# Layernorm, softmax-weighted attention and an integer-weight MLP on one core: block 0's rows in four transfers, its bias seeds on TensorE, the weight check on 16-bit copies, and six low halves moved to GpSimd

## What is computed

```
xn   = layernorm(x)                               # (2, 4096, 256)
h    = tanh(xn @ W1.T + b1);  s = h @ w2 + b2     # one score per token
e    = exp(s - max(s));  ctx = cumsum(e*xn)/cumsum(e)
out1 = tanh(concat(ctx, xn) @ Wc.T + bc)
out2 = (silu(xn @ wg.T/127) * (xn @ wu.T/127)) @ wd.T/127   # wg, wu 768x256, wd 256x768, integers -127..127
y    = x + out1 + out2
```

## Time and profile before

| | us |
|---|---|
| median of 3 runs (lowest, highest) | 399.24 (398.85, 399.65) |
| the profiled execution | 400.47 |
| its span, first to last instruction | 398.6 |
| TensorE busy in the span | 389.4 |
| VectorE, ScalarE, GpSimd busy | 295.6, 252.4, 198.2 |

### The profile page before, as it was taken

The page is one execution under the profiler, slowest core; times in us unless marked ns, Lnnn a source line. Parts: engine busy times, 40 slices in busy tenths (PEclk is TensorE's granted clock), DMA queues, the critical chain, the costliest instruction groups (busy, mean ns, idle before and its releaser), DMA issues.

```text
span 398.6 us, 7885 instructions
## 1 busy us (share of the span) xinstructions
PE 389.4 (98%) x2741; PEld 270.6 (68%) x2741; DVE 295.6 (74%) x629; ACT 252.4 (63%) x469; POOL 198.2 (50%) x257
## 2 busy tenths in 40 slices
PE   7979999999999999999999999999999999999995
PEld 3546766675667488677686876767758677686765
DVE  5998899999785889897666846689766776745351
ACT  4988787999797666975536574456353644626250
...
DMA packets 54612, 36.44 MB, mean 91 GB/s; under 512 B 31651, under 2 KB 49956, under 8 KB 54565
## 3 DMA queue, kind: packets, MB, share of 16 engines
...
...
## 4 chain that ended last, share of the span: by engine, by line
PE 91%; ACT 3%; DVE 3%; issue 1%; DMA 1%; DVEq 0%; ACTq 0%
PE bank L659 43%; PE bank L695 38%; PE bank L715 9%; ACT rows L879 1%; DMA xres<-in_x 1%; ACT xnat L809 0%; ACT ex L845 0%; DVE stats L913 0%; DVE bank L1053 0%; DVE bank L1068 0%; ACT sg L838 0%; PE bank L652 0%; DVE wide L1073 0%; DVE xnat L983 0%; PE bank L1288 0%
## 5 line engine op out<-in xcount | busy, mean ns | idle before, releaser
L695 PE MATMUL bank<-xt,narrow 128*128 128x512 f16 x768 | 176.7, 379 | 0.1
L695 PEld LDWEIGHTS bank<-xt,narrow 128*128 128x128 f16 x768 | 75.2, 98 | 77.3 <-DVE erT L1035 0.6
L659 PE MATMUL bank<-narrow,xt 128*128 128x256 f16 x768 | 94.8, 277 | 1.8 <-ACT bank L792 1.8
L659 PE MATMUL bank<-narrow,wide 128*128 128x256 f16 x792 | 96.3, 273 | 0.0
L659 PEld LDWEIGHTS bank<-narrow,xt 128*128 128x128 f16 x768 | 76.1, 100 | 19.3 <-ACT bank L792 2.2
L659 PEld LDWEIGHTS bank<-narrow,wide 128*128 128x128 f16 x792 | 77.4, 98 | 9.4
L838 ACT ACTIVATE sg<-bank 128x512 f32<-128x512 f32 x96 | 56.6, 594 | 39.7 <-PE bank L695 37.2
L1190 POOL TENSOR_TENSOR wide<-ex,wide 128x512 f16<-128x512 f32 x32 | 41.2, 1301 | 71.7 <-ACT wide L859 71.7
L1073 DVE TENSOR_TENSOR wide<-bank,wide 128x512 f16<-128x512 f32 x90 | 60.5, 682 | 20.7 <-ACT wide L845 19.1
L1068 DVE SCALAR_TENSOR_TENSOR bank<-bank,sg 128x512 f32<-128x512 f32 x96 | 65.4, 692 | 13.8 <-PE bank L695 13.0
L845 ACT ACTIVATE wide<-bank 128x512 f16<-128x512 f32 x90 | 53.1, 594 | 33.8 <-DVE bank L1068 32.7
...
## 6 DMA issues: line engine op xcount, KB each, us to landing
...
xt<-xt SPq DMA_TRANSPOSE x56, 2.5
wide<-in_wg SPq DMA_DIRECT2D x1, 768.0 KB, 5.9
wide<-in_wu SPq DMA_DIRECT2D x1, 768.0 KB, 7.5
wide<-in_wd SPq DMA_DIRECT2D x1, 768.0 KB, 10.2
...
```

The lines of the kernel that those rows point to most:

```text
L659: return pe.matmul(dst, lhs, rhs, start=False, stop=stop, skip_group_check=True)
L695: mm = pe.matmul(b[:, :], pg.up(which, k, j), pg.xn(sx, k, tok), start=n == 0, stop=n == len(todo) - 1)
```

## The change

1. **Block 0's x.** It came as two transfers of 256 KB (one issued by SyncE, one by ScalarE) and now comes as four of 128 KB (two by each). The biases and w2 are issued by ScalarE's queue behind them, and no longer by SyncE's. The statistics of the four tiles are taken in the order 0, 2, 1, 3, then all four are aggregated together. `WARM` goes from 13 to 12.
2. **Block 0's seeds.** `Ss` of block 0 is gone from ScalarE; TensorE writes the bias with two f32 matmuls of one row and 256 columns per pair, ahead of the pair's `S`.
3. **The integer checks.** They read the f32-sized integer weights, on ScalarE (four passes, `Kg` and `Kd`) and VectorE (`Ku`, `Ke`). They now read the f16 copies that GpSimd has made: VectorE clears the sign bit of wg and wu together (`Kg`, 3072 values), takes maxima of halves (`Kh` 1536, `Ku` 768), the same for wd (`Kd` 1536, `Ke` 768), and ScalarE compares the 768 left of each (`Kx`, `Ky`).
4. **Block 0's low halves.** For the six (0, j), `H` writes its f32 product into unused SBUF in place of the bank, which so comes free at `H`; `Hh` reads it there, and GpSimd makes the low half (`Hm`) instead of VectorE's `Hl`.
5. The planner's start times, some due times and the needs follow, so all orders are computed anew.

```diff
-BEGIN = {TE: 8.3, SE: 6.5, VE: 8.9, PO: 1.0, SY: 12.0}
+LOW_ON_POOL = tuple((0, j) for j in range(KH))
+BEGIN = {TE: 7.6, SE: 5.8, VE: 8.1, PO: 1.0, SY: 12.0}
...
             def scores(i, pr):
                 b = bank_of(pg, "S", i, pr)
-                pe.wait_ge(a_ss, pg.nth("Ss", i, pr))
+                if i or pg.wide:
+                    pe.wait_ge(a_ss, pg.nth("Ss", i, pr))
+                else:
+                    open_bank(pe, pg, "S", i, pr)
+                    for t in range(2):
+                        pe.matmul(b[:, t * D:(t + 1) * D], ups[:, :], b_row[:, 0:D],
+                                  start=t == 0, stop=False, skip_group_check=True)
...
-            elif kind in ("Kg", "Kd"):
-                w, done = (wg32, 0) if kind == "Kg" else (wd32[:, WD_SHARE:], 2)
-                act.wait_ge(s_wg if kind == "Kg" else s_wd, 16)
-                if done + n:
-                    act.wait_ge(a_ok, done + n)
-                beyond = rows[:, :, :, :].rearrange("p r k t -> p (r k t)").bitcast(BF16)[:, 0:w.shape[1]]
-                act.activation(beyond, w.bitcast(I32), ACT.Relu, bias=limit[:, 0:1], scale=-1.0 if n else 1.0,
-                               accum_out=guard[:, 2 + done + n:3 + done + n]).then_inc(a_ok, 1)
+            elif kind in ("Kx", "Ky"):
+                n, up = (0, 1.0) if kind == "Kx" else (1, 1.0 / WD_DOWN)
+                act.wait_ge(v_k2, 5 if n else 3)
+                if n:
+                    act.wait_ge(a_ok, n)
+                act.activation(beyond(), largest(2 * n), ACT.Relu, bias=limit[:, 0:1], scale=up,
+                               accum_out=guard[:, 2 + n:3 + n]).then_inc(a_ok, 1)
...
+        def stats_first(dve):
+            for t in (0, 2, 1, 3):
+                dve.wait_ge(s_x0[t], 16)
+                ins = dve.bn_stats(stats[:, t, :], xres[:, t, :])
+            ins.then_inc(v_bn, 2)
+            dve.wait_ge(v_bn, 2)
+            for t in range(4):
+                ins = dve.bn_aggr(mv[:, t, :], stats[:, t, :])
+            ins.then_inc(v_mv, 2)
...
+            elif kind in ("Kg", "Kd"):
+                first, n, w = (0, 4, narrow[:, 0:2 * n_int]) if kind == "Kg" else (2, 2, wd16)
+                dve.wait_ge(g_w, 2 if kind == "Kg" else G_W)
+                if kind == "Kd":
+                    dve.wait_ge(v_k2, 3)
+                dve.tensor_scalar(largest(first, n).bitcast(U16), w.bitcast(U16), NO_SIGN, None,
+                                  ALU.bitwise_and).then_inc(v_k2, 1)
+            elif kind == "Kh":
+                dve.wait_ge(v_k2, 1)
+                dve.tensor_tensor(largest(0, 2), largest(0, 2), largest(2, 2), ALU.max).then_inc(v_k2, 1)
             elif kind == "Ku":
-                dve.wait_ge(s_wu, 16)
-                check_reduce(dve, 6, wu32.bitcast(I32), AX.X).then_inc(v_k, 1)
+                dve.wait_ge(v_k2, 2)
+                dve.tensor_tensor(largest(0), largest(0), largest(1), ALU.max).then_inc(v_k2, 1)
...
+            elif kind == "Hm":
+                pool.wait_ge(a_h, pg.nth("Hh", i, k))
+                m = KH * i + k
+                pool.tensor_tensor(half(pg.h(1, m, slice(0, BLK))), up_full(i, k), half(pg.h(0, m, slice(0, BLK))),
+                                   ALU.subtract).then_inc(g_h, 1)
```

More of the change, by code:

```diff
@@ L113, in closing @@
         return ("Ct" if seeded(i, x) else "Ca"), i, x
+    if kind == "Gu" and (i, x) in LOW_ON_POOL:
+        return "H", i, x
     return CLOSES[kind], i, x
@@ L157, in due_times @@
             for n, i in enumerate(blocks):
-                lead = 6.0 if i == FIRST_T else 10.0
+                lead = 9.0 if i == FIRST_T else 10.0
                 due["B", i, 0], due["B", i, 1] = first - lead + 2.0 * n, first - lead + 1.0 + 2.0 * n
@@ L161, in due_times @@
                     due["Lx", i, 0] = first - 18.0 + 2.0 * n
-            root = first - (8.5 if FIRST_T in blocks else 8.5)
+            root = first - (11.5 if FIRST_T in blocks else 8.5)
             due["R", g, 0] = root
@@ L173, in due_times @@
             due["Xl", i, pr] = end["Lb", i, pr] + 0.8
-            due["Ss", i, pr] = due["S", i, pr] - (1.6 if i or not pr else 0.6)
+            due["Ss", i, pr] = due["S", i, pr] - 1.6
             due["Th", i, pr], due["Sv", i, pr] = end["S", i, pr] + 0.1, end["S", i, pr] + 0.8
@@ L262, in needs @@
     if kind == "S":
-        return [(("Ss", i, x), 0), ((*turned, x), 0.8 if turned[0] == "Xl" and not wide else 0),
+        return [*([(("Ss", i, x), 0)] if i or wide else []), ((*turned, x), 0.8 if turned[0] == "Xl" and not wide else 0),
                 *([] if turned[0] == "Tx" else [(("Xh", i, x), 0)]), *([] if i else [(("W1l", 0, 0), 0.4)])]
@@ L267, in needs @@
     if kind == "Sv":
-        return [(("Th", i, x), 0)]
-    if kind == "Ss" and i == 0 and not wide:
-        return [(("Ea", 0, 0), 0), *([(("Xh", 0, 0), 0)] if x else [])]
+        return [(("Th", i, x), 0), *([] if i or x else [(("Ea", 0, 0), 0)])]
+    if kind == "Ss":
+        return [(("Ea", 0, 0), 0)]
     if kind in ("Gg", "Gu"):
@@ L279, in needs @@
         return [(("H", i, x), 0), *slot]
-    if kind == "Hl":
+    if kind in ("Hl", "Hm"):
         return [(("Hh", i, x), 0)]
     if kind == "D":
-        return [(("Hl", i, k), 0.2 * k) for k in range(KH)] + ([(("Ct", i, x), 0)] if seeded(i, x) else []) \
+        return [(("Hm" if (i, k) in LOW_ON_POOL and not wide else "Hl", i, k), 0.2 * k) for k in range(KH)] + ([(("Ct", i, x), 0)] if seeded(i, x) else []) \
             + [(("D", i, 0) if x else ("Wdh", 0, 0), 0)]
@@ L318, in may_precede @@
     kind, i, _ = st
-    return kind in WEIGHTS + ONCE or (kind in AHEAD and i < (1 if kind in ("Hh", "Hl", "D") else 2))
+    return kind in WEIGHTS + ONCE or (kind in AHEAD and i < (1 if kind in ("Hh", "Hl", "Hm", "D") else 2))
 class Plan:
@@ L410, in take_one @@
                 self.times.add(t)
-            elif opened(st) is None or self.bank_for(st, now) is not None:
+            elif opened(st, self.wide) is None or self.bank_for(st, now) is not None:
                 self.start(e, st, now)
@@ L752, in tensor_step @@
                 pe.wait_ge(a_b, 1)
-                pe.matmul(bank_of(pg, "Kp", 0, 0)[:, 0:1], ones[:, :], guard[:, 8:9], start=True,
+                pe.matmul(bank_of(pg, "Kp", 0, 0)[:, 0:1], ones[:, :], guard[:, 4:5], start=True,
                           stop=True).then_inc(p_ok, 1)
@@ L1067, in vector_step @@
                 dve.wait_ge(p_u, pg.nth("Gu", i, n))
-                dve.scalar_tensor_tensor(out=dst, in0=b[:, :], scalar=pg.up_scale, in1=sg[:, m % SG_RING, :],
+                dve.scalar_tensor_tensor(out=up_full(i, n) if pg.low_on_pool(i, n) else half(dst), in0=half(b[:, :]),
+                                         scalar=pg.up_scale, in1=half(sg[:, m % SG_RING, :]),
                                          op0=ALU.mult, op1=ALU.mult).then_inc(v_h, 1)
@@ L1317, in _ @@
             dve.memset(warm[:, 0:BLK], 1.0).then_inc(v_set, 1)
+            dve.memset(ups[:, :], X_UP * W_UP)
             dve.memset(ones[:, :], 1.0).then_inc(v_set, 1)
-            for pr in range(2):
-                vector_stats(dve, 0, pr)
+            stats_first(dve)
             root_first(dve)
```

115 lines of the change are left out of this document (70 added, 45 removed).

## The result

| | before | changed |
|---|---|---|
| median of 14 runs each, us (lowest, highest) | 399.60 (398.85, 403.54) | 404.19 (401.72, 409.13) |
| ratio to before, 95% interval | | 1.0084 (1.0047 to 1.0121) |
| profiled execution: time, span | 400.47, 398.6 | 403.58, 401.8 |

The change made the kernel slower by 0.8%; the forecast was 396.2, and the range ended at 399.0. The ratio is over the fast executions alone: the four of the changed kernel from 408.75 to 409.13 us are left out of it, and with them the medians are 1.1% apart. The page of the changed kernel answers to the earlier trace rows: TensorE is as busy as before, in a span 3.2 us longer.

A forecast was written before the change was run, and what follows sets the result against it. TensorE, busy 389.4 of 398.6 us, was taken as the bound. Start +0.7, seeds −2.0 and between the blocks +4.3 made 3.0 us gained, taken off the median 399.24 to give 396.2; range 395.2 to 399.0.

The forecast's parts named there:

- Start, +0.7: Block 0's x in four pieces lets statistics and transposes start earlier: 0.7 us gained, bounds 0.08 to 0.77.
- Seeds, −2.0: Block 0's four new f32 seed matmuls lie on TensorE's dense path: 2.0 us lost (1.5 to 2.25).
- The rival with a second fall of the clock: Clock falls again despite shorter waits: gain only 0.4 us, 398.8 us; chance 0.08.
- 16-bit steps: VectorE's five new integer-check steps, priced at 1.05, 0.95, 0.55, 0.6 and 0.55 us.
- That rival: 16-bit steps run at 1.04 ns an element, 5.1 us more: 403.2 us, or 400.6 without a clock fall; chance 0.07.
- Between the blocks, +4.3: From block 0's gate and up to the branch: 4.3 us gained, 2.7 from the clock, 1.6 from less waiting.
- Nothing off TensorE costs anything there: From 32.93 to 394.5 us TensorE is busy for 361.51 of 361.57 us, so other engines cost nothing.
- A time saved before 32.93 reaches the end one for one: Early savings carry fully to the end, as all work behind 32.93 us is dense on TensorE.
- The cover worked out for the last Hm: Behind the branch, GpSimd's last low half ends at 38.2, with 1.6 us to spare for block 0's D.
- The case of a new wait behind the branch: Late last Hm or block 3's DMA transposes, grouped with partial gains: 0.5 to 2 us, 396.7 to 398.2; chance 0.2.

The follow-up runs named there:

- part 2 alone: Kernel before with only block 0's seeds as four one-row f32 matmuls on TensorE, run twice: 407.80 us (ratio 1.0162) and 406.21 us (1.0106).
- e3: Changed kernel with block 0's two seeds back on ScalarE and the four one-row matmuls gone from TensorE: 401.92 us, ratio 1.006.
- e4: Changed kernel, block 2's Xm behind block 3's root, block 12's second Xh later, block 0's seeds on ScalarE: 397.86 us (0.9946); again 398.02 (0.9952).
- e7: e4 plus four more constant f16 matmuls of 512 columns on TensorE ahead of the transposes: 397.85 us, ratio 0.9946.
- c1 to c3: The kernel before, unaltered, profiled three more times: 401.41, 402.45 and 400.87 us.
- e1: Changed kernel with GpSimd's first Xm of block 2 waiting until VectorE's root of block 3 is done: 402.68 us, ratio 1.0092.
- e2: Changed kernel with block 12's second Xh moved behind a later silu of block 5 in ScalarE's order: 403.05 us, ratio 1.0067.
- the three edits: The edits of e1, e2 and e3 put together in the changed kernel, run as e4: 397.86 us, ratio 0.9946; again 398.02 us, 0.9952.

## Why the prediction was wrong

The measured median is 8.0 us above the forecast. The step that failed most is the one that called the stretch behind 32.93 free of any cost off TensorE: VectorE's small steps meeting GpSimd's long ones, a wait that the old kernel had covered, and a third one that no run takes apart cost 4.5 us there. Then the seeds were priced at full clock only, which cost about 2.0 in the median (404.2 against 402.2 at full clock), and the whole gain of one profile was taken off the median, 1.1 too much. These make 7.6 of the 8.0. Term by term:

- *Start, +0.7.* Nearly right: the root's first step at 5.53 (forecast 5.4, before 6.12), transposes at 7.73 (7.63). Part 1 alone on the old kernel was worth 0.2 us at gate and up, and 0.2% at the end, within the uncertainty; that a part of the 0.7 was luck of the landing can't be excluded, as the transposes of kernels with four pieces began between 7.6 and 8.3.
- *Seeds, −2.0.* The matmuls themselves are as priced: 1.10 and 1.12 us a pair, gate and up of block 0 at 14.38 (14.14). The term failed in what it left out: it priced them at full clock only, and put no price on the matmuls around them running at the lower one. Of 24 executions, 10 recorded a mean clock below 0.988 and took 407.4 to 409.1 us; the two of them that were profiled were low while seeds and scores ran, at a cost of 5.5 and 4.5 us. With part 2 alone it was so in 13 of 18 (above 406), and in none of 34 with the seeds on ScalarE (e3, e4, e7). The rival with a second fall of the clock put it between the blocks, at 0.08.
- *16-bit steps.* Right: 0.96 for Kg (1.05 forecast), 0.95, 0.56, 0.56, 0.56. That rival is out.
- *Between the blocks, +4.3.* The events came as forecast: scores at 26.12 and 27.92 (25.9, 27.9), idle 0.34, 0.18 and 0.44 (0.1, 0.7, 0.5), on at 31.77 (31.7). Kg started at 13.35 and not at 12.3, which cost nothing here. But most of the 4.3 was the fall of the clock in one profile. The sum put it at 2.7, with 2.74 and 2.58 us that hold the end of the last matmul set against 1.31 that doesn't; against c1 to c3, which don't have it there, it is 2.5. The fall was also misread by a little: the mean of 0.66 from 26 to 27 us puts it at 26.3, after 0.7 us of idle time and not 1.03. Against executions without a fall the work ahead of the branch gained 2.9 − 2.5 = 0.4 us (an estimate, as none of that kind was profiled), not 3.0: waits and start gave 2.4, the seeds took 2.0. What failed is the step from the profiled execution to the median: I took the whole 3.0 off 399.24, as if the median held all of the profile's fall. At full clock the old kernel takes 397.7, so that with 0.4 gained it would have been 397.3, not 396.2.
- *"Nothing off TensorE costs anything there" (behind 32.93), and "A time saved before 32.93 reaches the end one for one".* Wrong, and the larger part at equal clock: 4.5 us. Block 3's root met GpSimd's Xm and Hm (2.8 us instead of 0.6, then 1.9 at `D`; e1). The old kernel has the same two Xm: there they ended at 36.73 and the root began at 36.69, so that it escaped them by its place in time, and two of the three long steps are beside them. ScalarE's wait for block 12's transfer, hidden before by 1.2 us of TensorE work, came out (2.1; e2). The third, 0.7 at 165, is again a seed by ScalarE, and I made no experiment on it alone. The cover worked out for the last Hm held (it ended at 37.70, `D` was due at 38.7), but I looked for what Hm delays on its own queue, and not for what it, and the Xm, delay on VectorE.
- *The sum at equal clock.* −0.4 ahead of the branch and +4.5 behind give +4.1; the group of full clock shows 402.2 − 397.7 = 4.5. The medians differ by 4.6 with the clock's losses on both sides.
- *The case of a new wait behind the branch* (0.2, up to 398.2) was the right kind, and it was sized as a single loss set against the full gain. Its two examples, the last Hm and block 3's transposes, are not what came.

What the three edits won against the old kernel is 0.4 us at full clock; most of their 2.0 to 2.8 us in the medians of the same chips comes with executions in which the clock fell less, which is seen in the table and not taken apart further. Open: what decides whether and where the clock falls in one execution, why one-row seeds go with the longer stretches, and the cause of the 0.7 us.
